# Output projection of an attention stage moved from shared PSUM bank pairs to a single PSUM bank, half as much at a time

## The reference, cut to what matters

```
x = x + attn_b(layernorm(x))
attn_b: q1, q2, k, v = x@Wq1, x@Wq2, x@Wk, x@Wv        (16 heads of 32)
        p  = softmax(causal(q k^T / sqrt(32)))          (for q1 and for q2)
        y  = p1 v - sigmoid(x@Wlam) * (p2 v)
        return y @ Wo                                   <- "the output"
```

## Time and profile before

| | us |
|---|---|
| median of 3 runs | 2510.14 |
| the 3 runs | 2508.71, 2510.14, 2511.02 |
| the profiled execution: its own time | 2508.71 |
| the profiled execution: its span | 2506.9 |
| TensorE busy in the span | 2141.1 (85%) |
| VectorE busy | 1484.2 (59%) |
| ScalarE busy | 888.7 (35%) |
| GpSimd busy | 814.6 (32%) |

### The profile page before, as it was taken

How to read it: one execution, slowest core, us unless ns; L and a number is a source line. 1 busy time by engine, 2 the same in 40 slices (tenths; PEclk the granted TensorE clock), 3 DMA queues, 4 the chain that set the end, 5 groups by cost and what they waited for, 6 DMA issues and landing times. The chain is left out here.

```text
span 2506.9 us, 32655 instructions
## 1 busy us (share of the span) xinstructions
PE 2141.1 (85%) x11664; PEld 896.6 (36%) x11664; DVE 1484.2 (59%) x1885; ACT 888.7 (35%) x1367; POOL 814.6 (32%) x395
## 2 busy tenths in 40 slices
PE   4888888869998978898898888898988776799998
PEld 2333333324444433433332323233333222344443
DVE  4877777744746443355556666656556665366544
ACT  2534353513433312333333333333332333244331
POOL 0755555520000000354455455454545554000000
PEclk7999999979999988999999999998999987899999
DMA  4000000020000002000100000000000000200000
GB/s 180 30 30 26 25 28 22 29 87 14 1 1 1 0 0 64 12 14 1 25 2 14 14 9 18 9 18 9 5 1 13 1 9 1 101 1 18 1 17 34
DMA packets 60765, 55.39 MB, mean 22 GB/s; under 512 B 36288, under 2 KB 44480, under 8 KB 60384
## 3 DMA queue, kind: packets, MB, share of 16 engines
q1 hardware_dynamic: 60640, 53.65, 6.9%
HBM read 43.02 MB, written 10.62 MB: 21 GB/s over the span
## 5 line engine op out<-in xcount | busy, mean ns | idle before, releaser
L1279 POOL TENSOR_TENSOR b_total<-b_total,b_prob 128x2048 f32<-128x2048 f32 (+3 forms) x160 | 515.5, 3222 | 545.5 <-ACT b_prob L1229 544.2
L1310 DVE TENSOR_REDUCE b_maxima<-psum 128x2 f32<-128x1024 f32 (+3 forms) x384 | 350.2, 954 | 440.1 <-PE psum L1078 296.4
L532 PE MATMUL psum<-hT,W 128*128 (+1 forms) x2048 | 452.4, 384 | 18.5 <-DMA W<-ternary 9.2
L1229 ACT ACTIVATE b_prob<-psum 128x1024 f32<-128x1024 f32 (+3 forms) x320 | 228.2, 765 | 472.9 <-PE psum L1113 305.5
L280 PE MATMUL psum<-hT,a_win 128*128 (+1 forms) x640 | 316.7, 646 | 6.1 <-DMA a_win<-in_w_inT 6.1
L532 PEld LDWEIGHTS psum<-hT,W 128*128 128x128 bf16 x2048 | 202.2, 99 | 267.7 <-issue 29.6
L1100 PE MATMUL psum<-b_qT,b_kT 32*128 32x512 f32 (+3 forms) x1536 | 189.9, 563 | 124.8 <-DVE b_maxima L1310 120.8
L667 DVE SCALAR_TENSOR_TENSOR f_h<-psum,f_sg 128x512 f32<-128x512 f32 x128 | 88.3, 691 | 226.1 <-ACT f_sg L592 224.4
L558 PE MATMUL psum<-W,f_hi 128*128 128x512 bf16 x512 | 197.3, 385 | 4.3 <-DVEq L653 3.5
L558 PE MATMUL psum<-W,f_lo 128*128 128x512 bf16 x512 | 197.1, 385 | 0.0
L280 PEld LDWEIGHTS psum<-hT,a_win 128*128 128x128 f32 x640 | 132.1, 210 | 164.8 <-issue 155.4
(11 more groups left out here) (158 smaller groups left out, 2729.3 us busy)
## 6 DMA issues: line engine op xcount, KB each, us to landing
a_stage<-in_w_guT SPq DMA_DIRECT2D x32, 256.0 KB, 2.7
ternary<-W SPq DMA_DIRECT2D x1, 6144.0 KB, 17.9
a_win<-in_w_inT SPq DMA_DIRECT2D x5, 1024.0 KB, 9.3
x<-in_x SPq DMA_DIRECT2D x4, 1024.0 KB, 9.1
a_stage<-in_w_pT SPq DMA_DIRECT2D x16, 256.0 KB, 2.6
b_wq<-in_wq SPq DMA_DIRECT2D x64, 64.0 KB, 2.6
b_lamT<-lam_rows SPq DMA_DIRECT2D x32, 128.0 KB, 2.7
W<-ternary SPq DMA_DIRECT2D x8, 512.0 KB, 7.9
```

What stands on the lines that cost most here:

```text
L532: last = pe.matmul(dst[:, :], W[:, k * 2 * HID + col:k * 2 * HID + col + P], hT[:, ds(i * (2 * KT * BLK) + (half * KT + k) * BLK, BLK)], s ...
L1229: act.activation(held(u, s)[:, 2 * a:2 * a + 2, off:BLK], pair_banks(("score", u, s, a))[:, :, off:BLK], ACT.Exp, scale=SCALE).then_inc(ex ...
L1279: pool.tensor_tensor(acc, acc, held(u, s)[:, :, off:BLK], ALU.add).then_inc(summed, 1)
L1310: dve.tensor_reduce(maxima[u % 2][:, :].rearrange("p (h q c) -> p h q c", h=HPT, q=QT)[:, 2 * a:2 * a + 2, qt, kc], pair_banks(("row", u, ...
```

## The change

The output becomes a fill job of one token tile: one matmul of 128x128 by 128x512 into bank 7, one VectorE addition of 512 columns (`finish`). There are 8 per turn instead of 4. They stand at step 9 place 1, step 10 place 0, step 11 place 0 and step 11 place 1 of a unit; `neg` stays at step 10 place 1, between them on the same bank. Tiles 0 to 3 are made in unit w=1 of the turn, tiles 4 to 7 in unit w=0 of the next. The last four of the last turn go to banks 0 to 3. The pairs are left to scores and rows. On VectorE, what belongs to place 0 is now taken out ahead of the row's maxima, and what belongs to place 1 behind them.

```
-FIRST_HALF = {(0, 0): "k0", ..., (7, 1): "q1", (10, 1): "neg0"}
+FIRST_HALF = {(0, 0): "k0", ..., (7, 1): "q1",
+              (9, 1): "out4", (10, 0): "out5", (10, 1): "neg0", (11, 0): "out6", (11, 1): "out7"}
-               (10, 1): "neg0"}
-OUT_AT = [{9: 2, 11: 3}, {10: 0, 11: 1}]
+               (9, 1): "out0", (10, 0): "out1", (10, 1): "neg0", (11, 0): "out2", (11, 1): "out3"}
...
+    if kind == "out" and r + w:
+        return ("out", r - 1 + w, n)
...
-EPILOGUE = [("den", UNITS - 1, 1)]
-EPILOGUE_BANKS = [7]
+EPILOGUE = [("den", UNITS - 1, 1)] + [("out", TURNS - 1, t) for t in range(TPB, QT)]
+EPILOGUE_BANKS = [7, 0, 1, 2, 3]
...
-ON_DVE = [job[0] == "norm" for job in JOBS]
+ON_DVE = [job[0] in ("out", "norm") for job in JOBS]
...
-        if out_in(_u, _i):
-            PAIR_USES.append(("out", *out_in(_u, _i), 0))
-PAIR_USES += [("out", TURNS - 1, two, 0) for two in (2, 3)]
...
+                elif kind == "out":
+                    _, r, t = job
+                    if t == 0:
+                        pe.wait_ge(wo_loaded[r % 2], 16 * (r // 2 + 1))
+                    pe.wait_ge(y_ready, 4 * r + 3 + t // TPB)
+                    last = pe.matmul(to, yT[r % 2][:, t * P:(t + 1) * P], wo_sl[r % 2][:, :], start=True, stop=True)
...
+                if kind == "out":
+                    _, r, t = job
+                    b, h = divmod(r, HT)
+                    if h:
+                        dve.wait_ge(fill_added, FREED_BY_DVE[NTH[("out", r - 1, t)]])
+                    dve.wait_ge(filled, n + 1)
+                    xt = x[:, (b * QT + t) * D:(b * QT + t + 1) * D]
+                    dve.tensor_tensor(xt, xt, src, ALU.add).then_inc(fill_added, 1)
...
+                    if (u, i, 0) in ENDING and ON_DVE[NTH[ENDING[u, i, 0]]]:
+                        finish(ENDING[u, i, 0])
                     if row_in(u, i):
                         row(*row_in(u, i))
-                    for place in range(2):
-                        if (u, i, place) in ENDING and ON_DVE[NTH[ENDING[u, i, place]]]:
-                            finish(ENDING[u, i, place])
-                    if out_in(u, i):
-                        add_out(*out_in(u, i))
+                    if (u, i, 1) in ENDING and ON_DVE[NTH[ENDING[u, i, 1]]]:
+                        finish(ENDING[u, i, 1])
```

More of the change, by code:

```diff
@@ L774 @@
 PARTS = {"k": KT, "q": KT, "v": KT}
-FIRST_HALF = {(0, 0): "k0", (2, 0): "den1", (2, 1): "k1", (5, 0): "den0", (5, 1): "q0", (7, 1): "q1", (10, 1): "neg0"}
+FIRST_HALF = {(0, 0): "k0", (2, 0): "den1", (2, 1): "k1", (5, 0): "den0", (5, 1): "q0", (7, 1): "q1",
+              (9, 1): "out4", (10, 0): "out5", (10, 1): "neg0", (11, 0): "out6", (11, 1): "out7"}
 SECOND_HALF = {(0, 0): "q0", (2, 0): "den1", (2, 1): "q1", (5, 0): "den0", (5, 1): "v0", (7, 1): "v1",
-               (10, 1): "neg0"}
-OUT_AT = [{9: 2, 11: 3}, {10: 0, 11: 1}]
-FILL_BEFORE_ROWS = tuple(range(12))
+               (9, 1): "out0", (10, 0): "out1", (10, 1): "neg0", (11, 0): "out2", (11, 1): "out3"}
 NORM_AT = {(3, 0): 0, (4, 0): 1, (6, 0): 2, (7, 0): 3}
@@ L839, in row_in @@
     return divmod(n, NR) if n < UNITS * NR else None
[L842 to L848, removed]
 PAIR_USES = [("row", *divmod(n, NR), a) for n in range(LEAD) for a in range(2)]
@@ L898, in phase_attention @@
         y_copied, y_ready = sem("y_copied"), sem("y_ready")
-        out_done, out_added = sem("out_done"), sem("out_added")
         turn_ready, high_kept = sem("turn_ready"), sem("high_kept")
@@ L976, in _ @@
                 if 2 <= r + 1 < TURNS:
-                    sp.wait_ge(out_added, OUTS.index((r, 0)))
+                    sp.wait_ge(fill_added, FREED_BY_DVE[NTH[("out", r - 1, QT - 1)]])
                     out_weights(r + 1)
@@ L1056, in take_pair @@
                         pe.wait_ge(row_max, (u * NR + s) * 2 + a + 1)
-                    elif kind == "out":
-                        pe.wait_ge(out_added, OUTS.index((u, s)) + 1)
                     else:
@@ L1081, in row @@
                             last.then_inc(row_done, 1)
[L1083 to L1092, removed]
             def scores(u, s):
@@ L1146, in _ @@
                         weigh(*divmod(u * NS + i - 1, NS))
-                    if i in FILL_BEFORE_ROWS and (u, i, 0) in PART_AT:
+                    if (u, i, 0) in PART_AT:
                         fill(*PART_AT[u, i, 0])
@@ L1150, in _ @@
                         row(*row_in(u, i))
-                    if i not in FILL_BEFORE_ROWS and (u, i, 0) in PART_AT:
-                        fill(*PART_AT[u, i, 0])
                     if (u, i, 1) in PART_AT:
                         fill(*PART_AT[u, i, 1])
-                    if out_in(u, i):
-                        output(*out_in(u, i))
             weigh(UNITS - 1, NS - 1)
@@ L1159, in _ @@
                 fill_all(job)
-            for two in (2, 3):
-                output(TURNS - 1, two)
             pe.wait_ge(y_copied, UNITS * CQ)
             pe.wait_ge(fill_copied, FREED_BY_ACT[-1])
-            pe.wait_ge(fill_added, FREED_BY_DVE[-1])
             for turn in range(CQ):
@@ L1356, in finish @@
             def finish(job):
-                n = NTH[job]
+                n, kind = NTH[job], job[0]
                 src = bank[JOB_BANK[n]]
[L1359 to L1371, removed]
+                if kind == "out":
[6 more added lines that the diff above has]
+                    dve.tensor_tensor(xt, xt, src, ALU.add).then_inc(fill_added, 1)
+                else:
+                    _, blk, t = job
+                    dve.wait_ge(high_kept, blk * TPB + t + 1)
+                    dve.tensor_tensor(norm.half(blk, 1, t), src.rearrange("p (k t) -> p k t", k=KT),
+                                      norm.half(blk, 0, t), ALU.subtract).then_inc(fill_added, 1)
             def early_stats(part):
                 if part == 0:
-                    dve.wait_ge(out_added, OUTS.index((HT, 0)))
+                    dve.wait_ge(fill_added, FREED_BY_DVE[NTH[("out", HT - 1, QT - 1)]])
                 for t in (2 * part, 2 * part + 1):
@@ L1427, in _ @@
             take(UNITS - 1, 1)
-            for two in (2, 3):
-                add_out(TURNS - 1, two)
-            dve.wait_ge(out_added, len(OUTS))
+            for job in EPILOGUE:
+                if ON_DVE[NTH[job]]:
+                    finish(job)
+            dve.wait_ge(fill_added, FREED_BY_DVE[-1])
             nper = 10
```

## The result

The changed kernel takes 2536.91 us, median of 4 runs (2527.31 to 2537.87); the kernel before took 2509.43 in 4 (2506.22 to 2511.02). The ratio is 1.0103, with a 95% interval of 1.0077 to 1.0129: about 1% slower. I had forecast 2510.4 us, within 2503 to 2516. The profiled execution has a span of 2535.6 us instead of 2506.9, 28.7 us more.

The account below looks back on a forecast made before the run. TensorE's instructions in order, plus its waits for VectorE's maxima, bound the kernel. 1.1 + 1.8 + 1.0 - 0.5 = +3.4 us, with -3.1 for the clock: +0.3, so 2510.4 us, range 2503 to 2516.

Parts of the forecast that it names:

- The wrong step: Step 10 of w=0: `negate` takes 1.09 us on VectorE without delay, and `out5` is added by 1358.34.
- A second step: Unit 15: the last outputs stand beside GpSimd's sums and cost nothing (0 to 1 us).
- Single outputs cost 0.19 us per pair more on TensorE: Output matmuls: two single outputs hold TensorE for 2.06 us against 1.87 for a pair, +0.19 per pair.
- steps 9 to 11 of w=0 lose a little: Units 2 to 12 with w=0: each loses 0.18 us, +1.1 us for six units.
- Unit 14 loses 1.8 by back-to-back outputs: Unit 14, no `row` between the outputs and `neg`: unit 15 starts 1.8 us late, between 0 and 1.8.
- `out0` is free in the wait of w=1: Step 9 of w=1: `out0`, 1.03 us, lies inside the wait of `scores` behind `take` and costs nothing.
- The clock comes back in two of six: w=1 units: the fall to clock 0.50 behind the long wait goes away in two of six, -3.1 us.
- the clock comes back everywhere: Rival: outputs cut all six w=1 waits and none has a slow stretch behind it; 2504.3 us, chance 0.23.
- bank 7 is the new bound: Rival: bank 7 returns later than 2.02 us at three w=0 places, 39 times; 0.25 more gives 2520 us; chance 0.2.
- The four terms of 2.02: Bank 7's return after a single output starts: matmul 1.08, VectorE's start 0.10, addition 0.69, signal 0.15 us.
- The end: Four last outputs cost TensorE the same 5.63 us; the last addition takes 0.69 instead of 1.22: -0.5 us.

Follow-up runs that it names:

- experiment 1: Changed kernel with the addition of step 9's output tile put behind `negate` in step 10 on VectorE: 2518.99 us, ratio 1.0045.
- experiment 2: Changed kernel with GpSimd's sum of step 10 in w=0 units cut from 256 to 8 columns per head: 2519.09 us, ratio 1.0045.
- experiment 3: Kernel before with GpSimd's sum of step 10 in w=0 units cut to 8 columns per head: 2509.13 us, ratio 0.9998.
- experiment 4: Kernel before with two scratch tiles of 512 columns written by VectorE ahead of `negate` in step 10 of six w=0 units: 2534.98 us, ratio 1.0105.
- experiment 5: experiment 2 with GpSimd's sums of steps 8 and 9 of unit 15 cut to 8 columns as well: 2505.53 us, ratio 0.9995.
- experiment 6: experiment 1 with unit 15's outputs moved late, two tiles to step 11 and two to the epilogue: 2520.37 us, ratio 1.0054.
- experiment 7: Kernel before with the first pair output of w=1 units 1 to 13 moved from step 10 to step 9: 2496.47 us, ratio 0.9953.
- experiment 8: experiment 7 with unit 15's pair outputs late, in step 11 and ahead of the last denominators: 2495.02 us, ratio 0.9949.

## Why the prediction was wrong

**The wrong step.** "`out5` to 1357.50. VectorE runs `negate` first, 1.09 us [...]; no delay. `out5` is added by [...] 1358.34." I carried over 1.09 us for `negate` from a place where its last subtraction started 0.53 us ahead of GpSimd's sum, to a place 0.08 us behind it. It took 3.2 us (1357.17 to 1360.39), the addition behind it ended at 1361.30, not 1358.34, and `neg` waited 1.93. I had seen the like in the earlier trace rows, where an operation of `take` starts 0.29 us behind a sum of 3.54 us and takes 3.80, and took it as a given of that place and not as what happens to any two-input instruction beside a sum. The replay followed TensorE and VectorE and left GpSimd out, because it was not near being the bound.

A second step failed in the same way: "In unit 15 itself the last outputs stand beside those sums and cost nothing (0 to 1 us)." Up to the start of its step 11 unit 15 is 7.5 us longer, because the output of step 9 waits 8.17 us for a `take` that stands behind two sums.

**What it set off.** The collision itself is 12.8 us of the 28.7 (shown, experiments 1 to 3). In units 6 and 12 the wait of 1.93 us, and in unit 14, where no row stands in front of it, one of 2.69, has a stretch of clock 0.50 behind it, 7.0 us, which went with the wait in experiments 1 and 2; experiment 4 shows such a stretch behind a wait of 2.62 us in six units of six. Unit 15 adds 7.5 by a collision of its own (shown, experiment 5), which depends on when things arrive there: experiments 1, 2, 4 and 6 have it, the kernel before and experiments 3, 7 and 8 don't.

What goes with it can be read in the ten traces, though no run changed it on purpose. In step 5 of unit 15 VectorE makes a row of the next layer norm and GpSimd starts a sum of 2048 columns (below, sums that follow each other are merged into one line). In the kernel before the row is through before the sum starts:

```profile
2077.46 0.55 DVE L1397 TENSOR_SCALAR b_early_rows<-x,b_e_mv,b_e_inv 128x512 f32<-128x512 f32 x1 [0.16 <-DVE b_yT L1347]
2078.05 13.84 POOL L1279 TENSOR_TENSOR b_total<-b_total,b_prob 128x2048 f32<-128x2048 f32 x3 [5.67 <-ACT b_prob L1229]
```

In the changed kernel the sum is first, and the row takes 4.49 us:

```profile
2100.22 9.44 POOL L1255 TENSOR_TENSOR b_total<-b_total,b_prob 128x2048 f32<-128x2048 f32 x2 [4.47 <-ACT b_prob L1205]
2100.80 4.49 DVE L1373 TENSOR_SCALAR b_early_rows<-x,b_e_mv,b_e_inv 128x512 f32<-128x512 f32 x1 [0.16 <-DVE b_yT L1323]
```

The row starts 4.06 us into the step in every trace. The sum, which waits for the step's exponentials, starts after 4.64 us in the kernel before and experiments 3, 7 and 8; after 3.48 in the changed kernel and experiments 1, 4 and 6; and after 4.04 in experiments 2 and 5, 0.01 to 0.02 us ahead of the row. Wherever the sum is first, `take` stands behind sums later on (in experiment 5 these are short). The sum is late where a stretch of clock 0.50 lies on the step: in the first four traces it has begun before the step starts (2073.27 to 2076.69 in the kernel before), in experiments 2 and 5 it begins 0.65 us into it, and in the other four there is none. How the late row carries on to `take`, three steps behind, was not tried. One of the changed kernel's four runs took 2527.31 us and the others 2537, which would fit a unit 15 without the collision; there is no trace of that run.

**Point by point.**

- Single outputs cost 0.19 us per pair more on TensorE, and steps 9 to 11 of w=0 lose a little: right, +0.08 to +0.15 per unit in experiment 2 against +0.18.
- Unit 14 loses 1.8 by back-to-back outputs: right, 1.67 in experiment 2; none of it was hidden.
- `out0` is free in the wait of w=1: right, `scores` behind it did not come later at full clock. Five of the seven units have 0.6 us more in step 9, where the clock is now down already while the output runs (2.05 us in unit 5 of the changed kernel, instead of 1.08 in unit 4).
- The clock comes back in two of six: wrong in kind, nearly right in size. It fell in all six; but in units 1 and 9, where it had been down for 6.8 us, it was down for 3.4, and in units 5 and 11 the other way round. The w=1 units are 1.7 us shorter in steps 9 to 11, against 2.1 forecast; that the sizes agree is luck, since no fall went away.
- Rival "the clock comes back everywhere": wrong with a single output, right in four of six with a pair (experiment 7). Read as one on unbroken gaps, the rule on the Trainium skill's page "TensorE: Matmul & The Clock Gate", section "HAM oscillation", does not hold here: with an output of one tile in the middle the clock fell in six of six. The kernel before could have told me, as in unit 15 the clock falls at 2073.27 behind a wait of 2.01 us (2070.80 to 2072.81).
- Rival "bank 7 is the new bound": slower was right, and so was one of its three places. Bank 7 came back 3.82 us after `out5` started (1357.54 to 1361.36) instead of 2.02, so `neg` waited 1.6 us more than forecast, but at one place in seven units and not at 39. The four terms of 2.02 held (the matmul 1.13 us, the addition 0.69); what was added is the addition's wait behind a `negate` that was held up.
- The end: the last addition took 0.69 instead of 1.22, right, worth 0.5.

## What to carry to other kernels

The replay with measured durations was good to a tenth of a microsecond per unit in the places where nothing was moved next to a GpSimd sum. Before carrying a duration to a new place, look at what runs beside it on every engine that can hold it up, GpSimd above all, and write down the margin: here 0.53 us of margin on an instruction of 0.19 us was worth 20 us of 2510. And when a wait is found that nothing shortens, fill it with as much work as it holds: in experiment 7 that gave 0.5%, and the granted clock stayed at 1.00 behind the wait in four places of six.

## What the runs showed of the hardware that was not expected

- A subtraction of 32 columns with both inputs in SBUF took 2.31 us when it started 0.08 us behind a GpSimd addition of 2.34 us, and 0.19 us otherwise; the GpSimd addition was not lengthened. Of the 64 additions of outputs in the changed kernel, with one input in PSUM, 21 started inside a sum, and none took more than 0.69 us.
- A wait of TensorE of 2.62 us (experiment 4) cost 2.65 us in its step and 1.5 us in the next, at a clock of 0.50, in six units of six. The wait of 1.93 us in the changed kernel did so in two of six.
- In unit 15 an instruction with one input in SBUF (the row of the next layer norm, shown above) took 4.49 us when it started 0.58 us behind a sum, and 0.55 when it was through before the sum. In the kernel before the next such row started in the middle of a sum (2084.30, the sum at 2082.72) and took 3.22.
